# A decoder's experts: weights loaded as 32x32 squares and turned by VectorE instead of TensorE

## What is computed

```
gates = einsum('bsd,ed->bse', x, gate_w)           # 16 experts
scores = sigmoid(gates); inds = top_k(scores + expert_bias, 8)
combine = scores of the chosen, divided by their sum, times 2.826, zero elsewhere
hg = einsum('bsd,eid->bsei', x, w_gate)            # w_gate, w_up: [16, 256, 256] = [expert, hidden i, feature d]
hu = einsum('bsd,eid->bsei', x, w_up)
ye = einsum('bsei,edi->bsed', silu(hg) * hu, w_down)   # w_down: [16, 256, 256] = [expert, feature d, hidden i]
y = einsum('bsed,bse->bsd', ye, combine) + the same for one shared expert
x = x + y
```

## Time and profile before

| | |
|---|---|
| Median of 3 runs | 2176.65 us (2174.35 to 2184.87) |
| The profiled execution: its own time | 2172.58 us |
| its span, first to last instruction | 2170.7 us |
| mean clock granted to PE over the span | 0.939 of full speed |
| busy: PE, DVE, ACT, POOL | 90%, 62%, 31%, 7% of the span |
| experts' stage | from about 1562 us to the end |
| DMA in the whole span | 43.47 MB, 43181 packets |

### The profile page before, as it was taken

One profiled execution on the slowest core, in us unless ns is written; L12 is line 12 of the kernel. 1 busy time (PEld: TensorE's weight loads), 2 busy tenths in 40 slices (PEclk: granted clock), 3 DMA queues, 4 the chain that ended last, 5 costly groups with the idle time before them and its releaser, 6 DMA issues. The chain is left out here.

```text
span 2170.7 us, 42812 instructions
## 1 busy us (share of the span) xinstructions
PE 1951.1 (90%) x16627; PEld 1634.7 (75%) x16627; DVE 1337.9 (62%) x3573; ACT 673.5 (31%) x1539; POOL 159.4 (7%) x121
## 2 busy tenths in 40 slices
PE   4999999688577999999999977877899999999998
PEld 3887887566356888888888864556788888888887
DVE  3566555366638787777877835764565555555554
ACT  2444435234223113212302204443533323323232
POOL 1000000110100000000000006560100000000000
PEclk9999999889768999999999988998899999999999
DMA  3000000100460000000000011000000000000001
GB/s 119 1 1 0 0 0 1 39 15 10 94 110 1 1 0 0 0 0 0 0 0 0 1 43 54 0 0 25 26 30 16 29 14 29 14 29 14 29 15 39
DMA packets 43181, 43.47 MB, mean 20 GB/s; under 512 B 3906, under 2 KB 42338, under 8 KB 43106
## 3 DMA queue, kind: packets, MB, share of 16 engines
q1 hardware_dynamic: 43106, 42.44, 7.3%
HBM read 40.34 MB, written 2.10 MB: 20 GB/s over the span
## 5 line engine op out<-in xcount | busy, mean ns | idle before, releaser
L2198 PE MATMUL f_out<-f_ko,f_gel 128*128 128x256 f32 x1024 | 243.9, 402 | 6.6 <-DVE f_gel L2355 6.6
L2198 PEld LDWEIGHTS f_out<-f_ko,f_gel 128*128 128x128 f32 x1024 | 207.2, 204 | 38.9 <-DVE f_gel L2355 7.3
L2623 DVE TENSOR_TENSOR m_act_up<-m_silu,m_up 128x512 f32<-128x512 f32 x136 | 93.6, 688 | 213.5 <-PE m_up L600 205.8
L2550 ACT ACTIVATE m_silu<-m_gate 128x512 f32<-128x512 f32 x136 | 81.5, 599 | 271.2 <-PE m_gate L600 271.2
L2609 DVE SCALAR_TENSOR_TENSOR g_x<-m_y,m_combine,g_x 128x256 f32<-128x256 f32 x272 | 118.9, 480 | 51.7 <-PE m_y L600 50.2
L229 ACT ACTIVATE a_prob<-a_score,a_neg_max 128x128 f32<-128x128 f32 x256 | 90.7, 367 | 167.0 <-DVE a_neg_max L219 166.9
L600 PE MATMUL f_act<-f_hT_pair_high,f_kiT_high 128*128 128x256 f32 x384 | 123.3, 321 | 0.3 <-ACT f_gel L2231 0.3
L2185 PEld LDWEIGHTS f_g<-f_col_hot,f_row_hot 64*128 64x128 f16 x4096 | 103.0, 94 | 26.8 <-issue 15.9
L2231 ACT ACTIVATE f_gel<-f_act 128x512 f32<-128x512 f32 x128 | 75.5, 598 | 126.2 <-PE f_act L600 107.7
L2185 PE MATMUL f_g<-f_col_hot,f_row_hot 64*128 64x32 f16 x4096 | 109.5, 176 | 2.8 <-DVE f_gel L2355 1.7
L2355 DVE SCALAR_TENSOR_TENSOR f_gel<-f_g,f_gel 128x512 f32<-128x512 f32 x128 | 87.7, 691 | 37.4 <-PE f_g L2185 34.8
(11 more groups left out here) (373 smaller groups left out, 4965.9 us busy)
## 6 DMA issues: line engine op xcount, KB each, us to landing
f_gel<-in_L_ffn_key_in SPq DMA_DIRECT2D x2, 2048.0 KB, 22.2
f_ko<-in_L_ffn_key_out SPq DMA_DIRECT2D x2, 2048.0 KB, 32.0
g_experts_w<-in_L_ffn_w_gate SPq DMA_DIRECT2D x16, 256.0 KB, 2.8
g_experts_w<-in_L_ffn_w_up SPq DMA_DIRECT2D x16, 256.0 KB, 3.0
g_experts_w<-in_L_ffn_w_down SPq DMA_DIRECT2D x16, 256.0 KB, 3.7
x_ctx<-in_ctx SPq DMA_DIRECT2D x8, 256.0 KB, 2.8
fp_wq_nat<-in_L_ffn_w_q SPq DMA_DIRECT2D x1, 2048.0 KB, 9.3
g_ctx_next<-in_ctx SPq DMA_DIRECT2D x8, 256.0 KB, 2.8
```

The costliest lines, as they stand in the source:

```text
L2198: last = pe.matmul(out_bank[:, t, :], gel[:, r, t * P:(t + 1) * P], ko[:, r, :], start=(r == 0), stop=(r == R - 1))
L2550: act.activation(silu[:, m, :], gate_bank[m][:, :], ACT.Silu).then_inc(silu_ready[m].sem, 1)
L2623: dve.tensor_tensor(act_up[:, m, :], silu[:, m, :], up_bank[m][:, :], ALU.mult) \
```

## The change

The routed experts' weights are no longer loaded as rows and transposed by PE. A 256x256 matrix is seen as 8 x 8 squares of 32x32. The loads put each square where its transpose has to lie: for the square with rows 32a to 32a+31 and columns 128k + 32b to 128k + 32b + 31, that is partitions 32b to 32b+31 of half k, columns 32a to 32a+31. One DMA covers one b and one k, that is 32 partitions x 8 squares x 32 elements (rows of 128 bytes); an expert has 3 x 4 x 2 = 24 of them (`load_blocks`). Then one DVE instruction per matrix transposes every 32x32 square in place of its grid (`turn_blocks`: 128x512, from w_blocks to w_turn, both in SBUF), and ACT and DVE make the high and low part from w_turn instead of from PSUM.

Squares have two buffers: `first_blocks` in `LateInputs`, filled with expert 1's before the last two stages, and `w_blocks`. SP issues expert 2's at the start of the stage and then, in a loop over two experts, those of expert e as soon as expert e-2 is turned. PE's `turn_weights` and the bank m_turn are gone. On DVE the turn of matrix g of the next expert stands at the start of group g, ahead of its first product; the low part stays where it was.

```diff
+    def load_blocks(self, sp, dst, weights, loaded):
+
+        n = self.BLOCK
+        for m, w in enumerate(weights):
+            blocks = w.rearrange("e (a i) (k b j) -> (e i) b k a j", i=n, k=KD, j=n)
+            for b in range(P // n):
+                for k in range(KD):
+                    sp.dma_start(dst[n * b:n * (b + 1), m, k, :].rearrange("i (a j) -> i a j", j=n), blocks[:, b, k, :, :]) \
+                        .then_inc(loaded, 16)
...
+        self.load_blocks(sp, self.first_blocks, self.first, self.blocks_loaded)
...
-            with sp.Fori(1, NE + 1) as e:
-                wait(sp, w_turned, e, 0)
-                for m, w in enumerate((w_gate, w_up, w_down)):
-                    sp.dma_start(w_nat[:, 2 * m:2 * m + 2, :],
-                                 w[bass.ds(e - 1, 1), :, :].rearrange("a o n -> (a o) n").rearrange("(t p) n -> p t n", p=P)) \
-                        .then_inc(w_loaded, 16)
-            sp.wait_ge(w_loaded, 48 * NE)
+            def load_blocks(e, n):
+                late.load_blocks(sp, w_blocks[n], [w[bass.ds(e - 1, 1), :, :] for w in (w_gate, w_up, w_down)], w_loaded[n])
+
+            load_blocks(2, 0)
+            with sp.Fori(1, NE // 2) as h:
+                for n in (1, 0):
+                    e = 2 * h + 2 - n
+                    wait(sp, w_turned, e - 2, 3)
+                    load_blocks(e, n)
+            for n in range(2):
+                sp.wait_ge(w_loaded[n], LOADED * NE // 2)
...
-        def turn_weights(pe, e, m):
-
-            pe.wait_ge(w_loaded, 48 * e)
-            wait(pe, w_low, e, m)
-            for k in range(KD):
-                for t in range(2):
-                    last = pe.transpose(turn_bank[:, k * HID + t * P:k * HID + (t + 1) * P],
-                                        w_nat[:, 2 * m + t, k * P:(k + 1) * P], ident[:, :])
-            last.then_inc(w_turned.sem, 1)
...
-                if g < 3 and not last_one:
-                    turn_weights(pe, e + 1, g)
...
-                act.copy(wT[par][0][:, m, :, :].rearrange("p k n -> p (k n)"), turn_bank[:, :]).then_inc(w_high.sem, 1)
+                act.copy(wT[par][0][:, m, :, :], w_turn[:, m, :, :]).then_inc(w_high.sem, 1)
...
-                dve.tensor_tensor(low, turn_bank[:, :], high, ALU.subtract).then_inc(w_low.sem, 1)
+                dve.tensor_tensor(low, w_turn[:, m, :, :], high, ALU.subtract).then_inc(w_low.sem, 1)
+
+            def turn_blocks(e, par, m):
+                if m == 0:
+                    dve.wait_ge(w_loaded[par], (LOADED // 2) * (e + par))
+                dve.transpose(w_turn[:, m, :, :].rearrange("p k n -> p (k n)"),
+                              w_blocks[par][:, m, :, :].rearrange("p k n -> p (k n)")).then_inc(w_turned.sem, 1)
...
                 for g in range(GROUPS):
+                    if g < 3 and not last_one:
+                        turn_blocks(e + 1, 1 - par, g)
                     for m in range(2):
```

More of the change, by code:

```diff
@@ L1551, with __init__ @@
     HID = 256
-    def __init__(self, s, ctx_in, w_in, b_in, gate_w, gate_b, s_gate, s_up, s_down):
+    BLOCK = 32
+    LOADED = 16 * 3 * KD * (P // BLOCK)
+    def __init__(self, s, ctx_in, w_in, b_in, gate_w, gate_b, s_gate, s_up, s_down, w_gate, w_up, w_down):
         self.ctx_in, self.w_in, self.b_in, self.gate_w, self.gate_b = ctx_in, w_in, b_in, gate_w, gate_b
         self.shared = (s_gate, s_up, s_down)
+        self.first = [w[0:1, :, :] for w in (w_gate, w_up, w_down)]
+        self.first_blocks = s.sb("first_blocks", [P, 3, KD, self.HID])
+        self.blocks_loaded = s.sem("late_blocks_loaded")
         self.w_nat = s.sb("aligned_w", [P, 2, D])
@@ L2403, in stage_experts @@
     TAKEN = -3.0e38
+    LOADED = late.LOADED
     with ExitStack() as ctx:
         s = Scope(nc, ctx, "m")
-        gate_bias, xnT, route_bank, w_nat = late.gate_bias, late.xnT, late.route_bank, late.experts_w
+        gate_bias, xnT, route_bank = late.gate_bias, late.xnT, late.route_bank
+        w_blocks = [s.sb("w_blocks", [P, 3, KD, HID]), late.first_blocks]
+        w_turn = s.sb("w_turn", [P, 3, KD, HID])
         score = s.sb("score", [P, NB, NE])
@@ L2420, in stage_experts @@
         y_bank = [s.ps(f"y{n}", [P, 2 * D]) for n in range(2)]
-        turn_bank = s.ps("turn", [P, 512])
         ones_set = s.sem("ones_set")
@@ L2424, in stage_experts @@
         logits_exp = s.sem("logits_exp")
-        w_loaded = s.sem("w_loaded")
+        w_loaded = [s.sem("w_loaded"), late.blocks_loaded]
         w_turned = s.counting("w_turned", 3)
@@ L2566, in copy_weights @@
                 wait(dve, w_high, e, m + 1)
-                high, low = (w[:, m, :, :].rearrange("p k n -> p (k n)") for w in wT[par])
-                dve.tensor_tensor(low, turn_bank[:, :], high, ALU.subtract).then_inc(w_low.sem, 1)
+                high, low = (w[:, m, :, :] for w in wT[par])
+                dve.tensor_tensor(low, w_turn[:, m, :, :], high, ALU.subtract).then_inc(w_low.sem, 1)
[4 more added lines that the diff above has]
+                              w_blocks[par][:, m, :, :].rearrange("p k n -> p (k n)")).then_inc(w_turned.sem, 1)
             route_links.link(dve, dve.tensor_copy(score[:, :, :], route_bank[:, :, 0, :]))
@@ L2694, in decoder @@
                           a["L1_ffn_expert_bias"], a["L1_ffn_shared_gate_w"], a["L1_ffn_shared_up_w"],
-                          a["L1_ffn_shared_down_w"])
+                          a["L1_ffn_shared_down_w"], a["L1_ffn_w_gate"], a["L1_ffn_w_up"], a["L1_ffn_w_down"])
         stage_gated_attention(nc, x, ident, head_mask, a["L1_attn_Wq"], a["L1_attn_bq"],
```

## The result

The changed kernel takes 2153.37 us (median of 6 runs, 2152.06 to 2161.83). The kernel before took 2183.02 us beside it (median of 6 runs). The ratio of the two kernels is 0.9883, with a 95% interval of 0.9857 to 0.991. That is the ratio of the mean times, 2155.6 and 2181.1 us; the medians alone would give 0.986. When both were timed again, the medians were 2157.37 (6 runs) and 2179.4 us (11 runs), and the ratio was 0.9892 (0.9871 to 0.9914). The profiled execution of the changed kernel took 2153.32 us (span 2151.6, mean granted clock 0.938), against 2172.58 for that of before, at 0.939. That is 19.3 us less. The forecast was 2155 us, made of 19.5 us less on the profiled execution and 2 us for the median. The measured time is in the range, and the change made the kernel faster, as forecast.

What follows compares the result with a forecast made beforehand. TensorE's instruction count was taken to bound the experts' stage. Removing transposes gave -20.6 us, expert 0 +1.1, so -19.5 from 2172.6 to 2153.1; splitting the median's 4.1 us offset gave 2155 us, forecast's own range 2150 to 2158.

Steps and rivals of the forecast that it cites:

- The bound: Experts' stage, about 1562 to 2171 us: TensorE's instructions set the end; a saved microsecond of TensorE is one of the kernel.
- Price of what is removed: TensorE's transposes in 16 routed experts: 48 turns at 0.43 us elapsed each, 20.6 us saved.
- Price on VectorE: 48 transposes of 128x512 added to VectorE, taken at 0.69 us each, hidden except in expert 0.
- The upper bound of 3.5 us: Upper end for one 128x512 VectorE transpose, from RECIPROCAL at 1.75 us for 128x256.
- the cover: Groups 1 and 2 after expert 0: a VectorE transpose of up to 2.56 us costs TensorE nothing.
- The rival of long transposes: VectorE transposes of 3.5 us make groups 1 and 2 of 15 experts late: 28 us lost there, 2184; chance 0.06.
- Expert 0: Group 1, where VectorE also routes: TensorE waits for m_hidden_low, 1.1 us lost.
- The loads: Squares per expert: 12 us of SP issuing, 10 us of packets (5.3 to 19.2), hidden in some 49 us.
- The rival of 94 ns a packet: Slow squares: an expert's load takes 38.4 us and ends last, time 2215 us, 42 slower; chance 0.08.
- The rival with 0.14: DMA writes or new tile places stretch TensorE's matmuls by 1 to 2%: 6 to 12 us lost, 2159 to 2165.
- The 3 us of doubt on addresses: Shifted SBUF places of the two weight sets could change matmul pace in all experts: 3 us more or less.
- The median: Runs' median 4.1 us above the profiled execution; difference split, so 2155 us predicted from a sum of 2153.1.

Runs made afterwards that it cites:

- e1: Changed kernel with four 128x128 TensorE transposes put back at each of 48 places, results unread: 2179.06 us, ratio 0.9999 to the kernel before.
- x3: Changed kernel with one spare 128x1024 VectorE transpose ahead of each turn: 2158.17 us, ratio 0.9902 to the kernel before.
- x6: Changed kernel with one spare 128x2560 VectorE transpose ahead of each turn: 2199.4 us, ratio 1.0093 to the kernel before.
- e9: Changed kernel with expert 1's squares issued at the start of the experts' stage instead of two stages earlier: 2162.0 us (one run).
- e7: Changed kernel with the second set of turned weights and all tiles behind it 256 bytes per partition further: 2146.1 us (one run).

## Why the prediction was right

**The bound.** TensorE is full in the stage before and after, so each microsecond taken from it was one of the span. e1 shows it the other way round: with only the transposes back, the stage is 21.1 us longer, where 48 x 0.44 is 21.1.

**Price of what is removed.** 0.43 us a turn from the distance of blocks, 20.6 in all; measured 0.44 and 21.1. The stage became 19.9 us shorter, of which 19.4 lie behind the start of expert 0's last down products (574.31 against 554.87 us to the end), for 45 turns. The rows' own durations, 272 ns x 4 x 48 = 52 us, would have missed by a factor of 2.5.

**Price on VectorE.** Taken at 0.69 us, measured 0.70. By the Trainium skill, "VectorE: DVE Perf Modes", section "The three transpose paths", the estimate was 1.24 us for 512 columns; in the x3 kernel 1024 columns take that. The upper bound of 3.5 us was far too wide, yet the rows settled what mattered: the cover ends at 2.4 us in group 2 and at 2.2 in group 1 (2.56 forecast for both), between the x3 kernel's 1.8 and the x6 kernel's 3.35. The rival of long transposes was priced too low for it: at 3.35 us its sum gives 30 x 0.79 = 24 us in the routed experts, and x6 lost 34.

**Expert 0.** 1.1 us forecast for the wait; 1.02 measured. The announced place was right too: group 1, for m_hidden_low.

**The loads.** Announced: 12 us of issuing, 10 us of packets (5.3 to 19.2), hidden in a window of 49 us. Issuing takes 12.7. Packets at 12.3 ns are 6528 x 12.3 / 16 = 5.0 us an expert, just below the lower bound of 5.3 (13 ns), and each load lands 1.9 us after its issue. So the last one lands some 15 us after the first issue, in the announced 12 to 30. The rival of 94 ns a packet was far off. The rule that speaks for it is that of the Trainium skill, "DMA: Bandwidth & Descriptors", Specifications: at least 512 bytes for the full rate. The loss of rate is in the trace: for the same bytes the DMA share rose from 0.07 to 0.15, since a byte costs about twice as much in packets of 128 bytes as in 1 KB. It costs no time here, because the load stays hidden, and no packet below 512 bytes costs more than 12.3 ns. What I had not weighed is that the danger came from the other term: four times the issues cost 204 us, twice the packets none.

**Pace of TensorE.** The rival with 0.14 fell: the groups without a turn are 8.37 and 8.45 us at a DMA share of 0.15, as they were at 0.07 (8.38, and 8.90 less 0.45). e1 shows it without that subtraction: 8.88 and 8.80 us with small packets, 8.90 and 8.81 with the old loads. The 3 us of doubt on addresses were not needed.

**The median.** The sum is for the profiled executions, whose granted clocks were 0.939 and 0.938: 19.5 forecast, 19.3 measured. That the median came within 2 us of the 2155 is partly luck. Executions of the changed kernel alone spread over 13 us, its median was 2157.37 when timed again, and the kernel before, taken at 2176.65 for the forecast, had medians of 2183.02, 2181.09 and 2179.4 later. The stage that was changed repeats, with 589.0 and 589.1 us in two profiles; what varies lies in the stages ahead, which the prediction treated as fixed.

## What to carry to other kernels

Price work that leaves TensorE by the distance between the blocks around it with and without it, never by its rows, and only where the engine doesn't wait: four transposes gave 0.44 us in the full stage, and twelve gave nothing in the one with gaps. Here a transpose could be moved to DMA and VectorE because VectorE's idle time ahead of what TensorE needs, read to the last consumer, exceeds one pass; what had to fit into the time of an expert was the number of issues times 0.5 us, not the packets. An in-order engine that takes over such a step also takes over its wait for data, so the first load has to be placed early. And a wait of TensorE can cost more than its length, since the granted clock can be lower behind it.

## What the runs showed of the hardware

- A packet from HBM to SBUF takes 10.1 ns of a DMA engine for 64 bytes, 12.3 for 128, and 47 for 1 KB, so per byte the small ones are 3.4 and 2.1 times as dear. Sizes between 128 bytes and 1 KB were not run. An issue on SP takes about 0.5 us for 64, 128 or 256 packets, and 0.73 for 512.
- Behind a pause of 6.56 us TensorE's 128x512 matmuls first started 0.43 us apart and not 0.23, at a granted clock of 0.50, so that 14 of them took 6.00 us instead of 3.2 (e9).
- VectorE's transpose in 32x32 squares of fp32, SBUF to SBUF, takes 0.70 us for 128x512, 1.24 for 128x1024 and 2.84 for 128x2560, close to 1.04 us for 1000 columns with 0.17 on top. ScalarE's copy of 128x512 takes 0.62 us out of SBUF, in the rows of w_turn above; out of PSUM it took 0.59 in the kernel before.
- Executions of the changed kernel differ by up to 13 us (2148.99 to 2162.03), those of the kernel before by up to 16.5 (2169.25 to 2185.72). Windows of 390 to 572 us, in the second profile of the changed kernel and then in e7:

```profile
390.00:572.00 182.00, 142.46 (x1878) 107.84 (x1879) 103.13 (x163) 64.31 (x114) 17.82 (x23) 0.85 0.07 19
```

```profile
390.00:572.00 182.00, 136.61 (x1936) 104.07 (x1936) 106.80 (x172) 65.06 (x115) 17.99 (x25) 0.90 0.07 19
```

  The program of this stage, the chunked cross attention, is the same in both, and the granted clock is 0.85 and 0.90. From SP's first load for it to the first for the next stage are 582.92 - 393.74 = 189.18 us in one and 570.66 - 393.39 = 177.27 in the other. That is 11.9 of the 15.1 us by which the experts' stage starts apart, at 1570.27 and 1555.18. Whether the lower clock is the cause or follows from something else was not tried. In the experts' stage itself, from 1600 to 2050 us, both have 1.00.
